# Attention block with its causal masks moved from TensorE to VectorE, and PV of the diagonal two steps late

## The reference

```python
h = layernorm(x) * (1 + ca) + sa
q = rotary((h @ Wq + bq)); k = rotary(h @ Wk + bk); v = h @ Wv + bv      # 16 query heads, 4 key/value heads of 64
logits = q @ k.T / 8                                                     # 2048 tokens
logits = where(tril, logits, -1e30)
x = x + ga * (softmax(logits) @ v @ Wo + bo)
x = x + gb * experts(layernorm(x) * (1 + cb) + sb)                       # 8 experts, the best 2 of each token
```

## Time and profile before

| | |
|---|---|
| median of 3 runs | 1443.35 us (1442.36 to 1443.93) |
| profiled execution, span of its instructions | 1441.1 us |
| PE busy | 1325.4 us, 92% |
| DVE busy | 953.8 us, 66% |
| ACT busy | 588.5 us, 41% |
| POOL busy | 563.4 us, 39% |
| mean granted TensorE clock | 0.963 |

### The profile page before, as it was taken

The page is one execution under the profiler, slowest core; times in us unless marked ns, Lnnn a source line. Parts: engine busy times, 40 slices in busy tenths (PEclk is TensorE's granted clock), DMA queues, the critical chain, the costliest instruction groups (busy, mean ns, idle before and its releaser), DMA issues.

```text
span 1441.1 us, 19077 instructions
## 1 busy us (share of the span) xinstructions
PE 1325.4 (92%) x6864; PEld 834.6 (58%) x6864; DVE 953.8 (66%) x1834; ACT 588.5 (41%) x1229; POOL 563.4 (39%) x541
## 2 busy tenths in 40 slices
PE   3699999987999998799999879999995699999998
PEld 2455555544555554455555445555543588888888
DVE  4677777676787776668777676877778644444444
ACT  2444544543454453444444444444453322232222
POOL 4454347353444645345445414644643301111110
PEclk9799999999999999899999989999998699999999
DMA  5000000000000000000000000000001001010101
GB/s 128 1 1 1 1 1 0 2 0 2 1 0 1 0 1 0 2 1 1 1 1 1 0 1 1 1 1 0 1 0 44 0 7 39 0 40 4 29 16 30
DMA packets 18449, 13.02 MB, mean 9 GB/s; under 512 B 7104, under 2 KB 15680, under 8 KB 18368
## 3 DMA queue, kind: packets, MB, share of 16 engines
q1 hardware_dynamic: 11072, 9.58, 2.3%
q10 hardware_dynamic: 7296, 2.36, 0.7%
HBM read 10.88 MB, written 1.05 MB: 8 GB/s over the span
## 4 chain that ended last, share of the span: by engine, by line
PE 77%; DVE 14%; issue 3%; POOL 3%; ACT 1%; ACTq 1%; SPq 0%; DVEq 0%; POOLq 0%; another core or an unknown queue 0%
PE PS L1046 16%; PE PS L1105 12%; PE PS L999 11%; PE PS L1027 10%; PE PS L1119 8%; PE PS L1029 8%; DVE k_split L761 2%; PE PS L975 2%; PE PS L1055 2%; PE PS L1064 2%; PE PS L1012 2%; DVE full L788 2%; DVE part_max L772 2%; PE PS L983 2%; DVE q_split L758 1%
## 5 line engine op out<-in xcount | busy, mean ns | idle before, releaser
L772 DVE TENSOR_REDUCE part_max<-PS 128x1 f32<-128x512 f32 (+2 forms) x576 | 348.8, 620 | 127.6 <-PE PS L999 103.0
L601 ACT ACTIVATE full<-PS 128x512 f32<-128x512 f32 x384 | 224.9, 598 | 231.2 <-PE PS L1029 215.5
L1027 PE MATMUL PS<-QT,KT 128*128 128x512 f32 (+3 forms) x640 | 271.4, 424 | 20.4 <-issue 18.7
L999 PE MATMUL PS<-KT,QT 128*128 128x512 f32 (+3 forms) x656 | 273.0, 429 | 10.0 <-ACT QMT L581 4.7
L1029 PE MATMUL PS<-QMT,KT 128*128 128x512 f32 (+3 forms) x640 | 237.7, 371 | 0.0
L999 PEld LDWEIGHTS PS<-KT,QT 128*128 128x128 f32 x656 | 127.2, 197 | 158.4 <-DVE part_max L772 74.1
L464 POOL TENSOR_TENSOR full<-full 128x2048 f32<-128x2048 f32 x32 | 145.7, 4576 | 173.7 <-PE PS L1046 173.0
L610 ACT ACTIVATE diag<-PS 128x512 f32<-128x512 f32 (+3 forms) x256 | 111.3, 437 | 243.5 <-PE PS L1032 217.1
L1046 PE MATMUL PS<-full,V 128*64 128x512 f32 x768 | 210.2, 626 | 0.0
L494 POOL TENSOR_TENSOR rot_cos<-qkv_sb,cos_sb 128x320 f32<-128x320 f32 x72 | 69.9, 970 | 335.0 <-DVE qkv_sb L748 332.6
L1027 PEld LDWEIGHTS PS<-QT,KT 128*128 128x128 f32 x640 | 125.8, 197 | 106.0 <-issue 39.0
(11 more groups left out here) (116 smaller groups left out, 1748.3 us busy)
## 6 DMA issues: line engine op xcount, KB each, us to landing
full<-in_L_ffn_experts_w_dram SPq DMA_DIRECT2D x24, 256.0 KB, 3.1
out_dram<-XA SPq DMA_DIRECT2D x4, 256.0 KB, 2.3
wqkv<-in_L_attn_Wq_dram ACTq DMA_DIRECT2D x1, 512.0 KB, 4.0
bqkv<-in_L_attn_bq_dram ACTq DMA_DIRECT2D x1, 512.0 KB, 9.3
wo_sb<-in_L_attn_Wo_dram SPq DMA_DIRECT2D x1, 512.0 KB, 8.8
sin_sb<-in_k_sin_dram ACTq DMA_DIRECT2D x1, 512.0 KB, 8.2
full<-in_L_wmod_dram SPq DMA_DIRECT2D x1, 384.0 KB, 9.2
cos_sb<-in_k_cos_dram ACTq DMA_DIRECT2D x1, 256.0 KB, 9.1
```

Of the source, the lines that this page charges most:

```text
L601: nc.scalar.activation(full[:, k % QUADS, r, :], PS[:, bank, :], ACT.Exp).then_inc(probs_ready, 1)
L772: nc.vector.reduce_max(part_max[:, t, b:b + 1], PS[:, bank, 0:width], AX.X).then_inc(ring_dve, 1)
L999: last = nc.tensor.matmul(PS[:, bank, 0:w], QT[:, ch % 2, h, t * P:(t + 1) * P], KT[:, 0, b * BANK:b * BANK + w], start=True, stop=not las ...
L1027: nc.tensor.matmul(o, KT[:, 0, kt * P:(kt + 1) * P], QT[:, ch % 2, h, q0:BANK], start=True, stop=False)
```

## The change

Both mask matmuls go. For the maxima, VectorE's `tensor_tensor_reduce` adds a bf16 table (`causal_max`) to the scores in PSUM, writes the sums back and reduces in the same instruction, on the diagonal banks alone. For the exponentials, ScalarE takes the unmasked scores, and a new step `tri` has VectorE multiply the corner of both heads in `diag` by a table of 1 and 0 (`causal_keep`), with a minimum ahead of it. `tri` stands one step behind its scores in the order, and PV of the diagonal two steps behind instead of one; PV waits for `tri` (`diag_masked`), and so do `poolsum` of the diagonal and `diagsum`. The wait of ScalarE before it overwrites `diag` is now per tile. Two small tables move into space that is used elsewhere, and the bf16 identity goes. The core of the diff:

```diff
-                main += [("s", J, q, r, 0), ("s", J, q, r, 1)] + pending
+                step_of = TB * q + r + starts_at[J]
+                main += [("s", J, q, r, 0), ("s", J, q, r, 1)]
+                main += [x for due, x in pending if due <= step_of]
+                pending = [(due, x) for due, x in pending if due > step_of]
                 if r == 0 and q > 1:
...
                         main += [("quadsum", J, m, part) for m in range(2) for part in range(4)]
-                pending = [("pv", J, q, r)]
+                if q == J // PAIRS:
+                    soon = J == 0 and r == TB - 1
+                    main += [("tri", J, r)] * soon
+                    pending += [(step_of + 1, ("tri", J, r))] * (not soon) + [(step_of + 2, ("pv", J, q, r))]
+                else:
+                    pending.append((step_of + 1, ("pv", J, q, r)))
...
-        place(diag_steps(6) + tail_steps(6), 7.0, 7.48),
+        place(diag_steps(6) + tail_steps(6), 7.07, 7.5),
...
-                        pool.wait_ge(probs_ready, n.at["s", J, ch, TB - 1, m] + 1)
+                        pool.wait_ge(diag_masked, n.at["tri", J, TB - 1] + 1)
...
+                    if J > 0:
+                        act.wait_ge(pv_done, n.at["pv", J - 1, (J - 1) // PAIRS, r] + 1)
                     if r == 0 and J > 0:
-                        act.wait_ge(pv_done, n.at["pv", J - 1, (J - 1) // PAIRS, TB - 1] + 1)
...
                     if ch == 0:
-                        nc.vector.tensor_reduce(q_max[:, 0, t, 2 * (J % PAIRS) + m, HEAD:HEAD + 1],
-                                                PS[:, bank, 0:width], AX.X, ALU.max, negate=True).then_inc(ring_dve, 1)
+                        nc.vector.tensor_tensor_reduce(out=scores, in0=scores, in1=causal_max[:, BANK - width:BANK],
+                                                       scale=-1.0, scalar=-MASKED, op0=ALU.add, op1=ALU.min,
+                                                       accum_out=q_max[:, 0, t, 2 * (J % PAIRS) + m, HEAD:HEAD + 1])\
+                          .then_inc(ring_dve, 1)
+                    elif b == ch:
+                        nc.vector.tensor_tensor_reduce(out=scores, in0=scores, in1=causal_max[:, BANK - width:BANK],
+                                                       scale=1.0, scalar=MASKED, op0=ALU.add, op1=ALU.max,
+                                                       accum_out=part_max[:, t, b:b + 1]).then_inc(ring_dve, 1)
...
+                elif kind == "tri":
+                    _, J, r = x
+                    dve.wait_ge(probs_ready, n.at["s", J, J // PAIRS, r, 1] + 1)
+                    corner = diag[:, :, r, r * P:(r + 1) * P]
+                    nc.vector.scalar_tensor_tensor(out=corner, in0=corner, scalar=-MASKED,
+                                                   in1=causal_keep[:].broadcast_to([P, 2, P]),
+                                                   op0=ALU.min, op1=ALU.mult).then_inc(diag_masked, 1)
...
-                    if last_bank:
-                        last = nc.tensor.matmul(PS[:, bank, w - P:w], ident16[:], causal16[:, 0, :],
-                                                start=False, stop=True)
...
-                    if q == ch:
-                        last = nc.tensor.matmul(PS[:, bank, q0:q0 + P], ident16[:], causal16[:, 1, :],
-                                                start=False, stop=True)
...
-                    need(probs_ready, n.at["s", J, q, r, 1] + 1)
+                    if q == ch:
+                        need(diag_masked, n.at["tri", J, r] + 1)
+                    else:
+                        need(probs_ready, n.at["s", J, q, r, 1] + 1)
```

More of the change, by code:

```diff
@@ L58, in constants @@
         "k_ident": np.eye(P, dtype=np.float32),
-        "k_causal": np.stack([np.where(col <= row, 0.0, MASKED), np.where(row <= col, 0.0, MASKED)], 1)
-        .astype(np.float32),
+        "k_causal": np.concatenate([np.zeros((P, BANK - P)), np.where(col <= row, 0.0, MASKED),
+                                    np.where(row <= col, 1.0, 0.0)], 1).astype(np.float32),
     }
@@ L89, in weight @@
             return part * (3.78 if x[0] == "max" else 2.0)
-        return {"pv": 2.1, "qmax": 1.5, "proj": 3.0, "low": 3.0, "qk": 3.5, "poolsum": 0.01, "maxed": 0.25,
+        return {"tri": 0.0, "pv": 2.1, "qmax": 1.5, "proj": 3.0, "low": 3.0, "qk": 3.5, "poolsum": 0.01, "maxed": 0.25,
                 "diagsum": 3.3, "quadsum": 0.01, "sum": 2.8, "rowsum": 12.6, "norm": 2.8, "modulation": 0.0,
@@ L124, in block_kernel @@
     starts, pending = [], []
+    starts_at = np.cumsum([0] + [TB * (J // PAIRS + 1) for J in PAIR_STEPS])
     for J in PAIR_STEPS:
@@ L170, in block_kernel @@
     closing = tail_steps(-1)
-    body = [("values",)] + merge([(float(b), x) for b, x in zip(before, main)], [(begin[end], x) for x in pending],
+    body = [("values",)] + merge([(float(b), x) for b, x in zip(before, main)], [(begin[end], x) for _, x in pending],
                                  *side)
@@ L288, in block_kernel @@
         wmod_sb = full[:, 1].rearrange("p a b -> p (a b)")[:, 0:6 * E]
-        causal = full[:, 2, 0, 0:2 * P].rearrange("p (a b) -> p a b", b=P)
-        silu_c, bo_sb, gate_bo = (full[:, 2, 1, n * P:(n + 1) * P] for n in range(3))
+        causal = full[:, 2, 0:2].rearrange("p a b -> p (a b)")[:, 0:BANK + P]
+        silu_c, bo_sb, gate_bo = (full[:, 2, 1, n * P:(n + 1) * P] for n in range(1, 4))
         gate_abs, gate_sign = (full[:, 2, 2, n * 2 * E:(n + 1) * 2 * E].rearrange("p (a b) -> p a b", b=E)
@@ L306, in block_kernel @@
                                .rearrange("p (t x) -> p t x", x=NX) for n in range(3))
-        best = sb("best", [P, TILES])
-        tok_sum = sb("tok_sum", [P, TILES])
+        best, tok_sum = (full[:, 5, 3, 3 * TILES * NX + n * TILES:3 * TILES * NX + (n + 1) * TILES] for n in range(2))
         tok_wT = sb("tok_wT", [P, NX, TILES])
@@ L795, in step @@
                     if part == 0:
-                        dve.wait_ge(probs_ready, n.at["s", J, ch, TB - 1, m] + 1)
+                        dve.wait_ge(diag_masked, n.at["tri", J, TB - 1] + 1)
                         dve.wait_ge(quad_added, n.at["quadsum", J, m, TB - 1] // TB + 1)
@@ L996, in step @@
                     bank = ring_bank(x)
[L997 to L1000, removed]
-                    if last_bank:
-                        last = nc.tensor.matmul(PS[:, bank, w - P:w], ident16[:], causal16[:, 0, :],
-                                                start=False, stop=True)
-                    last.then_inc(ring_filled, 1)
+                    w = (t + 1) * P if b == ch else BANK
+                    nc.tensor.matmul(PS[:, bank, 0:w], QT[:, ch % 2, h, t * P:(t + 1) * P],
+                                     KT[:, 0, b * BANK:b * BANK + w], start=True, stop=True).then_inc(ring_filled, 1)
                 elif kind == "qmax":
```

19 lines of the change are left out of this document (10 added, 9 removed).

## The result

The changed kernel takes 1562.14 us (median of four runs, 1560.81 to 1564.32) beside 1443.33 us before it on the same chip (1442.36 to 1443.93): 1.0818 times the time, 95% interval 1.0803 to 1.0834. It is slower, as forecast, but by 118.8 us and not by 60: the time lies 4 us above the upper end of the range.

What follows compares the result with a forecast made beforehand. PE, busy 92% of the span, was taken as the bound, with DVE near it in stages 0 and 3. Per round -13.0 + 5.2 + 7.4 + 6.2 + 4.2 + 5.0 = +15.0 us, four rounds +60: 1503 us, range 1450 to 1558.

Steps and rivals of the forecast that it cites:

- What goes: All four rounds: 528 mask matmuls leave PE, gaining 13.0 us a round, 1.6 us a stage.
- VectorE's load: DVE in each round: `tri` 425 ns each, masked maxima 0.1 us more each, bringing DVE to 211 us of 259 us.
- Rival C: Masked maximum is two full passes: 31 us a round more on DVE instead of 6.4, 1539 us; chance 0.06.
- tri behind the quad sums: Stages 6 and 7: eight quad sums precede `tri` of tile 0; PE stands 6.2 us, and the round ends 4.2 us later.
- tri against GpSimd: Stages 4 and 5: `tri`, with two SBUF inputs, is blocked by GpSimd pairs; 7.4 us a round, bounds 0 and 18.
- The end of the round: Stage 7: first diagonal PV starts only after the quad sums, round ends 4.2 us later, plus about 2.5 us of slow clock.
- In the other stages DVE has the room: Outside stages 0 and 3, DVE's load costs nothing; those two stages were charged 5.2 us a round together.
- The clock: Half rate after the stalls of stages 6 and 7: 5.0 us a round, bounds zero and twice that.
- The sum: All terms give +15.0 us a round, +60 us over four rounds, 1503 us; chance 0.68.
- A: Stalls come mildly, `tri` mostly misses GpSimd pairs, clock stays: +4.6 us a round, 1462 us; chance 0.13.
- B: Two steps of delay suffice, PE never stands behind `tri`: -7.8 us a round, 1412 us; chance 0.09.

Runs made afterwards that it cites:

- the one-input form: Changed kernel with `tri` replaced by a maximum over the same 256 elements, one SBUF input, same place and waits, exponentials' mask missing from the output: 1524.77 us.
- `tri` unwaited: Changed kernel with `tri` writing to a scratch tile nobody reads; PV and the sums wait for the exponentials alone: 1440.21 us, 0.9972 of the kernel before.
- the quad sums spread: Changed kernel with the eight quad sums of stages 6 and 7 in threes behind `tri` of tiles 0, 1 and 2: 1526.94 us, 1.0561 of the kernel before.

## Why the prediction was right in kind and short in size

By stages of the second round, in us; the forecast is the prediction's terms put in their stages, with 1.6 us off each for its masks and 2.5 us of the clock in each of stages 6 and 7:

| stage | 0 | 1 | 2 | 3 | 4 | 5 | 6 | 7 | sum |
|---|---|---|---|---|---|---|---|---|---|
| forecast | +1.2 | -1.6 | -1.6 | +0.8 | +1.5 | +2.7 | +7.1 | +5.1 | +15 |
| measured | +2.1 | +0.6 | -0.6 | +4.2 | +3.9 | +4.5 | +12.0 | +2.6 | +29 |

- **What goes**: 13.0 forecast, 12.4 measured by the kernel without masks. The size is right, in part by luck: three stages gained next to nothing and stage 7 gained 4.4 us instead of 1.6, because a wait in it shrank that the prediction had left as it was.
- **VectorE's load**: `tri` 0.425 against 0.416 us bare, the masked maximum +0.1 against +0.14 us, VectorE 211 against 214 us a round. Right. Rival C (two passes) is out: 692 ns is one. By the Trainium skill (VectorE: DVE Perf Modes, Two Vector instructions with no wait between them) an instruction that writes out its accumulator is two; the trace agrees, and the second one takes 140 ns.
- **tri behind the quad sums**: the mechanism was right, at both places. Its size in stage 6 was 8.86 us, not 6.2. By the forecast the quad sums start 40.0 us into the stage, as in the earlier trace rows; they started at 44.2 (573.72 - 529.50). I put the 4.2 us down to the GpSimd pair across `low`: 3.55 + 4.58 us in place of 0.65 + 0.88 before, where it ran just behind the pair. The runs bear it out for 3.6 of the 4.2 us: in the two kernels without masks, which differ in the order, the quad sums start 39.1 and 42.7 us into the stage. The pair is there because the order moved: PV of stage 5's last diagonal tile now falls into stage 6, so the items put in at fractions of the stage slid, and `proj` with its rotary, and `low` behind it, fell on the other side of a step. In the list of before the pair stands ahead of the third projection of the stage, now behind it, and it starts 32.0 us into the stage instead of 24.8 (561.55 - 529.50 and 507.50 - 482.70). The prediction read the new order at the diagonals alone and took the rest from the old trace. That a pair across `low` blocks it was on view in the earlier trace rows.
- **tri against GpSimd**: 7.4 us a round forecast; the one-input form gives 37 us, 9.3 a round, of which some 5 are stalls and some 4 the clock. Stage 4 stalled 2.47 us (3.1 forecast), stage 5 1.4 and 1.5 us (1.4 and 2.9). The mechanism is right, both bounds held, and the stalls were charged somewhat too high; the clock behind them was left out.
- **The end of the round**: +5.1 forecast, +2.6 measured. PE stood 4.7 us before the first PV and worked at half clock behind it, as forecast. The rest came back in the middle of the stage, where PE stood 5.0 us before and 1.1 and 1.7 us in the changed kernel. The kernels without `tri` show the same (1.0 and 1.8 us with no mask, 1.1 and 1.6 with the maxima masked by VectorE), so it is nothing that `tri` does.
- **"In the other stages DVE has the room"**: wrong as a reason to charge nothing there. Room is a mean over a stage, and `tri` has a place in a queue. In stages 0 to 3 it stood behind reductions and cost PE waits of 1.2 to 2.2 us each; together these stages came out 7.5 us a round above the forecast (+6.3 against -1.2), of which 1.4 us are the clock of stage 0. This is the second step that failed: PE's idle time in these four stages grew by 9.8 us a round, where 5.2 were charged. In stage 3, with `tri` unwaited, the stage takes 26.5 us and not 30.3, at the same kinds of instructions on VectorE: the wait is the cost, not the load.
- **The clock**: 5.0 us a round forecast, between zero and ten. This step failed most. Over the four rounds PE was at work at half clock for 133.1 us in the changed kernel and for 36.6 us before (records of its work laid over the granted clock). Half of the difference is 48 us, 12 a round, above the upper bound. The prediction hung the clock on the two long stalls and gave stages 4 and 5, at most, as much again. In the second round the work at half clock grew from 3.1 to 5.9 us in stage 0, from nothing to 3.4, 5.4 and 8.5 us in stages 4, 5 and 6, and from 5.5 to 10.5 us in stage 7; no wait for `tri` in stages 4 and 5 was over 2.5 us. With both long stalls taken out (the quad sums spread) the work at half clock stayed at 130.9 us.
- **The sum**, over the four rounds: -49 for the masks, +113 of idle time of PE, +48 for the clock make +112 us, where the rounds grew by 120. The 8 us are not assigned; the -49 hold 4.5 us of clock of their own (27.6 us of work at half clock with no mask, 36.6 before). The forecast's sum had -52, then 92 for stalls and lost gain, and 20 for the clock. So of the 59 us by which the forecast missed the median, some 28 are the clock and some 21 the waits.
- **The rivals**: A (mild stalls, the clock stays) is out by the clock alone. B (two steps are enough) is out; it asked for waits under 4 us at the two places of the quad sums, and they were 8.9 and 4.7 us.

## What to carry to other kernels

Work that moves from a bound engine to one with idle time stands in that engine's queue, and whoever waits for it inherits all that was written ahead of it: price it item by item at its place, not by the engine's idle share. Where the work has a consumer on the bound engine, a stall can cost twice, once as time and once in the clock: here the short waits of stages 4 and 5 did, and those of stages 1 to 3 did not. Where an order is changed, read the neighbours again too: a GpSimd pair slid onto two VectorE instructions that it had missed before. Take the two halves of such a change apart: here the one fused into an instruction that ran anyway won 33 us, and the one that put a new instruction between two engines, to save 16, lost 117.

## What the runs showed of the hardware

- TensorE's clock fell in stages with short stalls too. Stages 4 and 5 of the second round had 0.96 and 0.91, with waits for `tri` of 2.47 us and of 1.4 and 1.5 us, and stages 1 to 3 kept 1.00 with waits of 1.2 to 2.2 us. Taking out the two long stalls of a round left the work at 1.2 GHz at 130.9 us (133.1 with them). Behind the stall of stage 6, 5.2 us of work ran at 0.50.
- A two-input VectorE instruction of 0.41 us took up to 2.45 us beside GpSimd instructions of 4.6 us; with one input, at the same place, never more than 0.423. A transpose with one SBUF input and 512 elements written to SBUF took 0.71 us beside them as elsewhere.
- A masked maximum with its sums written back to PSUM takes 692 ns for 512 columns, 5 ns more than a reduction that writes nothing back; beyond that it adds 140 ns for the accumulator.
